# One block for all stages of a perceiver layer: what moves where when the last cross-attention steps and the self-attention units share their queues

## The chip, the core and the metric

The kernel runs on one core of one Trainium2 chip. A core has TensorE (PE, matmuls and transposes; PEld is its weight load), VectorE (DVE), ScalarE (ACT), GpSimd (POOL) and SyncE (SP, which issues the DMAs). Each engine takes its instructions strictly in the order in which they are written, and waits on semaphores between them. The metric is the device time of the whole program in microseconds (us), lower is better; three runs gave 1323.09, 1324.57 and 1327.39 us, median 1324.57.

## The reference

Two batches of 256 rows with 256 channels (`x`) attend to 4096 context rows (`ctx`), then to themselves, then pass through a gated FFN whose activations and weights are rounded to FP4 in blocks of 16.

```python
x = x + xattn(layernorm(x), ctx)    # 16 heads of 64, softmax over 4096 keys, biases, output through Wo
x = x + attn(layernorm(x))          # 16 heads of 16, 256 keys; k and v come from latent_kv @ W_up
x = x + ffn(layernorm(x))           # 256 -> 704 -> 256, silu(gate) * up, fp4 on every input
# inside attn:
latent_kv = (x @ W_k + x @ W_v) @ W_down_kv          # 64 wide
scores = (q_h . k_rec_h) / sqrt(256) * exp(-0.01 * |i - j|)
```

## The kernel before, in words

The program has two blocks, one after the other; at the end of a block every engine waits for the others.

**Block 1, `cross_attention`.** 8 groups (2 batches x 4 groups of 4 heads) of 16 steps, N = 128 steps. Step n handles one head and 1024 keys: `scores(n + 1)`, four turns (`turn`, PE transposes of the softmax numerators) and four value products (`values`), with `p_high` on ACT and `p_low` on DVE splitting each turned tile into two parts. Steps 0 to N - 5 also project keys and values for step n + 4 (`project_k`, `project_v`), which POOL then splits (`split_piece`, `split_v`); the last four steps, N - 4 to N - 1, have no projection. In these four the kernel has two `post` transposes of the last group (step N - 2) and the building of the decay table on ACT. Batch 0's rows of `y` are complete some twelve steps before the end; the last group only adds to batch 1.

Behind step N - 1, in order: `post` 2 and 3 (transposes of the last group's outputs), the combination of the self-attention's k, v and down weights (L628, L635), `turn_o` and `project_o` (L508, L517), and `add_y` on DVE (L872). This is the last merge.

**Block 2, `self_attention_and_ffn`.** Norm of all four row tiles (bn_stats on DVE, a square root on ACT, L1412), transposes and projections (`x`, `lat`, `q`, `k`, `v`, 9 visits to the PSUM tile `saP`), then U = 32 units, one per batch and head. Loop index i on PE holds `scores(i)`, `turn(i - 2)`, `values(i - 3)`; DVE multiplies by the decay and takes the maximum (L1663, L1666), ACT does exp (L1495), the copy of the turned tile (L1503) and, for units 0 to 12, the masking of q for a head (`sa_qm`, L1505). Between the units DVE and POOL round the FFN weights to FP4 in six chunks: `WEIGHT_AT` says at which unit DVE does its parts of a chunk, POOL does four tensor operations per chunk (L1112 to L1118), and `TURN_AT` says at which i PE transposes it (L1269, L1275). DVE may not start chunk c before POOL has finished chunk c - 2. Behind the units stands the FFN: gate, up, rounding chains on DVE (`round_chain`), and down. `idle` (L1197) is a matmul whose result nobody reads.

## Time and profile before

| | |
|---|---|
| median of three runs | 1324.57 us |
| the profiled execution | 1324.31 us, of which its span 1322.6 us |
| busy share of the span | PE 97%, PEld 84%, DVE 67%, ACT 67%, POOL 72% |
| cross-attention, start to last value product | 0 to about 1149.9 us |
| last merge, norm, projections | about 1149.9 to 1178.1 us |
| units | 1178.1 to about 1270.8 us |
| FFN | about 1270.8 to 1322.6 us |

The page of the profile gives busy shares over the whole span. Of those 97% most is cross-attention, so the shares say little of the stages behind it; these are read from the timeline and from the busy times of short stretches.

### The profile page before, as it was taken

How to read it: one execution, taken by the hardware profiler on the slowest of the kernel's cores; microseconds unless marked ns; L12 is line 12 of the kernel's file. 1: busy time of each engine (PE TensorE's matmuls, PEld its weight loads, DVE VectorE, ACT ScalarE, POOL GpSimd, SP SyncE). 2: the span in 40 equal slices, each digit the busy share in tenths (PEclk: the TensorE clock that was granted, in tenths of full speed). 3: DMA queues.
4: the chain of work that ended last, by engine and by line, in shares of the span. 5: the costliest groups of instructions: out<-in, count | busy, mean ns of one | idle time of the engine just before them, and what ended most of it. 6: DMA issues, size and time to landing. Idle time of an engine off the chain costs nothing. (4 is left out here: it accounts for less than half of the span.)

```text
span 1322.6 us, 25021 instructions
## 1 busy us (share of the span) xinstructions
PE 1277.8 (97%) x9210; PEld 1107.2 (84%) x9210; DVE 881.7 (67%) x1408; ACT 881.7 (67%) x1721; POOL 947.9 (72%) x1096
## 2 busy tenths in 40 slices
PE   5899999999999999999999999999999999798998
PEld 5788888888888888888888888888888888567875
DVE  3666667666766677667666676667666766748557
ACT  3677776667767666777676776666777667548641
POOL 4877897789867976788778977898779777117310
PEclk9999999999999999999999999999999999989989
DMA  4010000000001001110000000000000001200000
GB/s 135 18 41 13 17 1 9 9 17 1 9 9 33 1 17 41 41 49 1 17 1 17 1 9 10 17 1 9 9 1 1 1 9 33 72 1 1 1 1 16
DMA packets 24904, 22.97 MB, mean 17 GB/s; under 512 B 4432, under 2 KB 24528, under 8 KB 24784
## 3 DMA queue, kind: packets, MB, share of 16 engines
q1 hardware_dynamic: 24784, 21.38, 5.3%
q8 instruction: 74, 1.21, 0.4%
q14 instruction: 46, 0.38, 0.1%
HBM read 20.85 MB, written 0.52 MB: 16 GB/s over the span
## 5 line engine op out<-in xcount | busy, mean ns | idle before, releaser
L684 ACT ACTIVATE pT_hi<-psT 128x512 fp32r<-128x512 f32 x512 | 293.4, 601 | 242.9 <-PE psT L437 239.6
L774 DVE TENSOR_TENSOR pT_lo<-psT,pT_hi 128x512 fp32r<-128x512 f32 x512 | 330.1, 685 | 103.1 <-ACT pT_hi L684 102.4
L768 DVE TENSOR_REDUCE negm<-psS 128x1 f32<-128x1024 f32 x256 | 311.4, 1217 | 20.5 <-PE psS L427 16.9
L336 POOL TENSOR_TENSOR kT<-kraw,khi 64x512 fp32r<-64x512 f32 x252 | 324.0, 1286 | 0.0
L647 ACT ACTIVATE prob<-psS,negm 128x1024 f32<-128x1024 f32 x256 | 285.5, 1115 | 1.0 <-DVE negm L768 1.0
L437 PEld LDWEIGHTS psT<-ident,prob 128*128 128x128 f32 x2048 | 230.2, 141 | 65.2 <-issue 36.8
L437 PE MATMUL psT<-ident,prob 128*128 128x128 f32 x2048 | 273.5, 276 | 3.8 <-DVE pT_lo L774 3.8
L453 PE MATMUL psO<-pT_hi,v 128*128 128x256 f32 x1024 | 268.7, 295 | 2.9 <-DVE pT_lo L774 1.2
L454 PE MATMUL psO<-pT_lo,v 128*128 128x256 f32 x1024 | 256.8, 282 | 0.0
L453 PEld LDWEIGHTS psO<-pT_hi,v 128*128 128x128 f32 x1024 | 194.7, 190 | 5.3 <-DVE pT_lo L774 2.9
L427 PE MATMUL psS<-kT,q_hi 64*128 64x512 f32 x1024 | 194.8, 416 | 3.4 <-ACT prob L647 2.0
L841 DVE TENSOR_TENSOR oT<-psO,olow 64x256 f32<-64x256 f32 x128 | 53.5, 418 | 214.9 <-ACT olow L745 214.9
L454 PEld LDWEIGHTS psO<-pT_lo,v 128*128 128x128 f32 x1024 | 195.7, 191 | 0.0
L330 POOL CAST khi<-kraw 128x512 fp32r<-128x512 f32 x126 | 76.9, 611 | 163.4 <-ACT kraw L657 160.5
L348 POOL TENSOR_TENSOR v<-vraw,v 128x512 fp32r<-128x512 f32 x124 | 159.7, 1288 | 9.9
L335 POOL CAST kT<-kraw 64x512 fp32r<-64x512 f32 x252 | 153.4, 609 | 15.5
L478 PE MATMUL psW<-wv_s,ctxT_hi 128*128 128x256 f32 x1000 | 160.7, 283 | 0.0
L465 PE MATMUL psW<-ctxT_hi,wk_s 128*128 128x512 f32 x496 | 145.9, 416 | 0.7 <-DVE oweighed L854 0.6
L478 PEld LDWEIGHTS psW<-wv_s,ctxT_hi 128*128 128x128 f32 x1000 | 138.0, 192 | 0.1
L427 PEld LDWEIGHTS psS<-kT,q_hi 64*128 64x128 f32 x1024 | 96.3, 184 | 41.3 <-issue 13.1
L427 PE MATMUL psS<-kT,q_lo 64*128 64x512 f32 x512 | 101.2, 391 | 0.0
L478 PE MATMUL psW<-wv_s,ctxT_lo 128*128 128x256 f32 x500 | 100.7, 283 | 0.0
(258 smaller groups left out, 1669.1 us busy)
## 6 DMA issues: line engine op xcount, KB each, us to landing
cst<-in_ctx_dram SPq DMA_DIRECT2D x12, 512.0 KB, 3.9
wraw<-in_L_xattn_Wk_dram SPq DMA_DIRECT2D x8, 256.0 KB, 2.7
wraw<-in_L_xattn_Wv_dram SPq DMA_DIRECT2D x8, 256.0 KB, 2.7
wraw<-in_L_xattn_Wq_dram SPq DMA_DIRECT2D x8, 256.0 KB, 2.6
wo<-in_L_xattn_Wo_dram SPq DMA_DIRECT2D x8, 256.0 KB, 2.7
oT<-in_ctx_dram SPq DMA_DIRECT2D x2, 512.0 KB, 5.5
prob<-in_ctx_dram SPq DMA_DIRECT2D x2, 512.0 KB, 4.7
ff_wdn<-in_L_ffn_w_down_dram SPq DMA_DIRECT2D x1, 704.0 KB, 7.5
```

The source lines that it names most:

```text
L335: pool.tensor_copy(kT[half, m // 2 % KRING, h, 0, :], raw[own, :]).then_inc(k_split, 1)
L336: pool.tensor_tensor(kT[half, m // 2 % KRING, h, 1, :], raw[own, :], khi[own, :].bitcast(F32), ALU.subtract).then_inc(k_split, 1)
L348: pool.tensor_tensor(v[:, m % VRING, :, :, 1, :], heads, v[:, m % VRING, :, :, 0, :].bitcast(F32), ALU.subtract).then_inc(v_lo, 1)
L427: last = mm(psS[:, qt, half * PIECE:(half + 1) * PIECE], q[rows, (h + half) % 2, h // 2, qt * P:(qt + 1) * P], kT[rows, n // 2 % KRING, h ...
L437: last = pe.transpose(psT[:, t % 2, k * S + qt * P:k * S + qt * P + P], prob[:, prob_slot(n, qt), (2 * t + k) * P:(2 * t + k + 1) * P], id ...
L453: mm(psO[:, 0:S], w, pT_hi[:, at, k * S:(k + 1) * S], start=(t == 0 and k == 0), stop=False)
L454: last = mm(psO[:, 0:S], w, pT_lo[:, at, k * S:(k + 1) * S], start=False, stop=(t == TB - 1 and k == 1))
L478: last = mm(dst[:, k * GD:(k + 1) * GD], x_[:, kt, keys], wv_s[:, a, kt, :], start=(j == 0 and kt == 0), stop=(j == 2 and kt == KT - 1))
L647: act.activation(prob[:, prob_slot(n, qt), :], psS[:, qt, :], ACT.Exp, bias=negm[:, g % 2, h, qt, c:c + 1], accum_out=lsum[:, g % 2, h, qt ...
L684: act.activation(pT_hi[:, i % PRING, :], psT[:, t % 2, :], ACT.Copy).then_inc(ph_ok, 1)
L768: dve.tensor_reduce(negm[:, g % 2, h, qt, c:c + 1], psS[:, qt, :], AX.X, ALU.max, negate=True)\
L774: dve.tensor_tensor(pT_lo[:, i % PRING, :], psT[:, t % 2, :], pT_hi[:, i % PRING, :].bitcast(F32), ALU.subtract).then_inc(pl_ok, 1)
```

## The change

The two blocks become one, and the tiles of the later stages are laid over tiles of the cross-attention that are dead by then. All stages therefore stand in one queue per engine, and work is put elsewhere in these queues:

- Batch 0's input norm: statistics on DVE in steps N - 12 and N - 11, the inverse root as 14 small POOL operations (`newton`) and the normalization as two POOL operations in step N - 7 (`input_norm(0)`). No square root on ACT is left here.
- Batch 0's projections and the combination of the k, v and down weights: in steps N - 4 to N - 1, through the PSUM bank `psW`. The first two units' scores, unit 0's maximum and exp: in step N - 1.
- The last merge: `post` 2 and 3, `turn_o`, `project_o` at i = 2, 3, 5, 6 of the unit loop; `add_y` at unit 7.
- Batch 1's norm at units 8 and 9 (DVE) and inside POOL's chunk 2; its projections at i = 11 to 15.
- The masking of q is done per batch: 3 DVE operations in step N - 2, one ACT operation in step N - 1 and 28 ACT operations in the units, of 256 columns each, where there were 3 DVE and 13 ACT operations of 512 columns.
- `idle` matmuls: 17 go before and in the first units; one comes at each of i = 32, 33, 34, four before `turn_xq(1)`, two before `turn_h(3)`. `hidden(1)` stands ahead of `normalize(1)`.

The PE queue from the last value products of step N - 1 on, before (psO is the value product's bank, oT and on the last group's outputs):

```order
L453 MATMUL psO<-pT_hi,v 128x256
L454 MATMUL psO<-pT_lo,v 128x256
L500 MATMUL psW<-ident,oT 128x128 x4
L500 MATMUL psS<-ident,oT 128x128 x4
L628 MATMUL psT<-ident,sa_w 128x128 x4
L635 MATMUL psT<-sa_wd,sa_wkvT 128x64 x4
L508 MATMUL psW<-ident,on 128x128 x4
L517 MATMUL psW<-wo,oweighed 128x256 x4
L81 UNCONDITIONAL_BRANCH
```

From there to the branch that ends the block there is nothing of the units. The PE queue of step N - 1 now (L858 is batch 0's v projection, L905 unit scores, L917 unit turns, L745 `post`):

```order
L699 MATMUL psO<-pT_lo,v 128x256
L858 MATMUL psW<-sa_wu,sa_latT 128x256 x2
L682 MATMUL psT<-ident,prob 128x128 x8
L905 MATMUL saS<-sa_kT,sa_qm 128x256 x2
L682 MATMUL psT<-ident,prob 128x128 x8
L698 MATMUL psO<-pT_hi,v 128x256
...
L905 MATMUL saS<-sa_kT,sa_qm 128x256 x2
L698 MATMUL psO<-pT_hi,v 128x256
...
L699 MATMUL psO<-pT_lo,v 128x256
L905 MATMUL saS<-sa_kT,sa_qm 128x256 x2
L745 MATMUL psW<-ident,oT 128x128 x4
L917 MATMUL saT<-ident,sa_p 128x128 x4
```

The scores of units 0 and 1 stand between the turns and value products of the step, and unit 2 directly behind its last product.

The POOL queue around chunk 2 of the weights, before (ff_win are the gate and up weights):

```order
L1118 TENSOR_TENSOR ff_win<-ff_wa,ff_wamax 128x768
L1112 TENSOR_TENSOR ff_wa<-ff_win,ff_wrs 128x768
L1114 TENSOR_TENSOR ff_wa<-ff_wa,ff_wm 128x768
L1116 TENSOR_TENSOR ff_wa<-ff_wa,ff_wm 128x768
L1118 TENSOR_TENSOR ff_win<-ff_wa,ff_wamax 128x768
L1112 TENSOR_TENSOR ff_wa<-ff_win,ff_wrs 128x768
```

and now (sa_l are the norm's small tiles, cst the normalized rows of batch 1):

```order
L632 TENSOR_TENSOR ff_win<-ff_wa,ff_wamax 128x768
L621 TENSOR_TENSOR ff_wa<-ff_win,ff_wrs 128x768
L529 TENSOR_SCALAR sa_l<-sa_l 128x2
L530 TENSOR_SCALAR sa_l<-sa_l 128x2
L533 TENSOR_TENSOR sa_l<-sa_l 128x2
L535 TENSOR_TENSOR sa_l<-sa_l 128x2
...
L537 TENSOR_SCALAR sa_l<-sa_l 128x2
L539 TENSOR_TENSOR sa_l<-sa_l 128x2
L548 TENSOR_SCALAR cst<-y,sa_mv,sa_l 128x256 x2
L628 TENSOR_TENSOR ff_wa<-ff_wa,ff_wm 128x768
L630 TENSOR_TENSOR ff_wa<-ff_wa,ff_wm 128x768
L632 TENSOR_TENSOR ff_win<-ff_wa,ff_wamax 128x768
```

Fourteen small operations and the two normalizations of batch 1 stand between the first and the second operation of chunk 2.

The diff, cut to its core:

```diff
+            def input_norm(b):
+
+                rows = slice(QT * b, QT * b + QT)
+                pool.wait_ge(lguess, 2 * b + 2)
+                newton(lv[:, rows], lw[:, rows], lt[:, rows], lr[:, rows], lroot, ROOT_OPS * b)
+                pool.wait_ge(lroot, ROOT_OPS * (b + 1))
+                for r in range(QT * b, QT * b + QT):
+                    pool.tensor_scalar(s_xn[:, r, :], y[:, r, :], s_mv[:, r, 0:1], lr[:, r:r + 1], ALU.subtract, ALU.mult)\
+                        .then_inc(sxn_ok, 1)
 
...
                                        ALU.add).then_inc(bo_ok, 1)
+                if n == N - 7:
...
+                pool.tensor_tensor(blocks(a), blocks(src), wide(wrs), ALU.mult).then_inc(wp, 1)
+                if c == 0:
+                    for k in range(2, 4):
+                        add_out(GP - 1, k)
+                if c == 2:
+                    input_norm(1)
+                pool.wait_ge(wq, wq_at[c, 6])
...
 
+            dims = lambda d: slice(d * P, (d + 1) * P)
+            rows_b = lambda b: slice(b * S, (b + 1) * S)
+
+            def idle(dst, count):
+
+                for _ in range(count):
+                    mm(dst, ident[:, :], sw[:, 0, 0, :], start=True, stop=True)
+
+            def turn_x(b, dst):
+                pe.wait_ge(sxn_ok, QT * (b + 1))
...
-                elif k == 14 and g + 1 == GP:
+                elif n == N - 4:
+                    turn_x(0, psW[:, :])
+                elif n == N - 3:
+                    combine_kv()
+                elif n == N - 2:
+                    pe.wait_ge(proj_ok, projected(0, "q"))
                     post(g, 0, psW[:, :])
+                elif n == N - 1:
+                    pe.wait_ge(proj_ok, projected(0, "k"))
+                    unit_v(0, psW[:, :])
                 if n + 1 < N and visit_first(n):
...
-                if g == GP - 1 and k == 14:
+                elif n == N - 3:
+                    project_lat(0, psW[:, :])
+                elif n == N - 2:
                     wait(pe, comb, 8 * g + 1)
                     post(g, 1, psW[:, :])
+                elif n == N - 1:
+                    unit_scores(0)
                 turn(n, 2)
...
+                elif n == N - 4:
+                    turn_kv()
+                elif n == N - 3:
+                    pe.wait_ge(proj_ok, projected(0, "lat"))
+                    unit_q(0, psW[:, :])
+                elif n == N - 2:
+                    wait(pe, comb, 8 * g + 2 * 1 + 1)
+                    unit_k(0, psW[:, :])
+                elif n == N - 1:
+                    unit_scores(1)
                 if early:
...
-            pe.wait_ge(comb, 8 * (GP - 1) + 2 * 1 + 1)
-            post(GP - 1, 2, psW[:, :])
-            pe.wait_ge(exp_ok, 2 * N)
-            post(GP - 1, 3, bank_S[0])
-            pe.wait_ge(tail.kv_ok, 1)
-            pe.wait_ge(pl_ok, 4 * N)
...
-            turn_o(GP - 1)
-            project_o(GP - 1)
+            for i in range(2, U + 3):
+                if i < U:
+                    unit_scores(i)
+                if i == LATE:
+                    pe.wait_ge(proj_ok, projected(0, "v"))
+                    post(GP - 1, 2, psW[:, :])
+                if i == LATE + 1:
+                    post(GP - 1, 3, bank_S[0])
+                if i == LATE + 3:
+                    turn_o(GP - 1)
+                if i == LATE + 4:
+                    project_o(GP - 1)
+                if i < U + 2:
+                    unit_turn(i - 2)
+                if turns_at(i) is not None:
+                    turn_w(turns_at(i))
+                if i in PROJECT_AT:
+                    kind = PROJECT_AT[i]
+                    same_bank_free(kind, 1)
+                    project[kind](1, saP[:, bank_of(kind, 1), :])
+                if i == 21:
+                    turn_out(0)
...
+                if i == U - 1:
+                    turn_xq(0)
+                if i >= U:
+                    pe.wait_ge(wt_ok, NG)
+                    idle(saP[:, 0, 0:D], 1)
+                if i >= 3:
+                    unit_values(i - 3)
+
+            gate(0)
+            turn_out(1)
+            up(0)
+            project_out(1)
...
+            pe.wait_ge(x1_ok, 2)
+            idle(saO[:, 1, 0, :], 4)
+            turn_h(0)
+            down(0)
+            pe.wait_ge(eg_ok, 2)
+            idle(saT[:, 0, 0, :], 4)
+            turn_xq(1)
...
+            residual(3)
+            pe.wait_ge(eg_ok, R)
+            idle(saT[:, 0, 0, :], 2)
+            turn_h(3)
+            down(3)
...
+                elif n == N - 4:
+                    projected_out(0, "x", psW[:, :])
...
+                elif n == N - 1:
+                    projected_out(0, "v", psW[:, :])
...
+                elif n == N - 3:
+                    projected_out(0, "lat", psW[:, :])
...
+                elif n == N - 4:
+                    wait(act, tail.kvT_ps, 1)
+                    act.activation(tail.wkvT[:, :, :].rearrange("p t n -> p (t n)"), psW[:, :], ACT.Copy)\
+                        .then_inc(tail.kvT_ok, 1)
+                elif n == N - 3:
+                    projected_out(0, "q", psW[:, :])
+                elif n == N - 2:
+                    projected_out(0, "k", psW[:, :])
+                elif n == N - 1:
+                    unit_exp(0)
                 wait(act, av_ok, 4 * n + 4)
...
-            o_out(GP - 1)
+                if n == N - 2:
...
+            for u in range(1, U + 2):
+                if u == LATE + 3:
+                    o_out(GP - 1)
+                if turns_at(u) is not None:
+                    weight_out(turns_at(u))
+                if u in PROJECT_AT:
+                    kind = PROJECT_AT[u]
+                    projected_out(1, kind, saP[:, bank_of(kind, 1), :])
+                if u < U:
+                    unit_exp(u)
+                if u >= 2:
+                    unit_turned_out(u - 2)
+                if u + 3 < U:
...
+                if n == N - 1:
+                    unit_max(0)
...
+                if n in (N - 12, N - 11):
+                    input_statistics(n - N + 12)
+                if n == N - 10:
+                    input_guess(0)
+                if n == N - 2:
+                    for i in range(3):
+                        own_rows(i)
                 out_sum(n)
...
-            for k in range(2, 4):
-                weigh_out(GP - 1, k, psW[:, :] if k == 2 else bank_S[0])
-                add_out(GP - 1, k)
-            add_y(GP - 1)
...
-            cols = lambda d: slice(d * P, (d + 1) * P)
-            idle(psO[:, 1, 0, :], 7)
-            pe.wait_ge(xn_ok, R)
-            for kt in range(KT):
-                step(("x", kt), turn_x(kt))
-            pe.wait_ge(proj_ok, at[("x", 1)] + 1)
-            pe.wait_ge(wc_ok, 1)
-            step(("lat", 0), product([(wc[:, kt, :], xnT[:, kt, :]) for kt in range(KT)]))
-            pe.wait_ge(w_in[2], 16)
...
-                if i in (2, 3):
-                    idle(psO[:, 1, 0, :], 5 if i == 2 else 1)
...
-                if i == 3:
-                    idle(psO[:, 1, 0, :], 4)
-                if i >= 3:
-                    values(i - 3)
...
+                if u >= 1:
+                    unit_max(u)
+                if u in (LATE, LATE + 1):
+                    weigh_out(GP - 1, u - LATE + 2, psW[:, :] if u == LATE else bank_S[0])
                 for c, op in weight_ops(u):
                     weight_op(c, op)
+                if u == LATE + 5:
+                    add_y(GP - 1)
+                if u in (LATE + 6, LATE + 7):
+                    input_statistics(QT + u - LATE - 6)
+                if u == LATE + 7:
+                    input_guess(1)
...
             round_chain(CHAIN_H[0], hh[:, 0, :], range(5))
             statistics(1)
             round_chain(CHAIN_H[0], hh[:, 0, :], range(5, 9))
+            hidden(1)
             normalize(1)
             dve.wait_ge(fxn_ok, 4)
             round_chain(CHAIN_X, input_rows(1), range(10))
-            hidden(1)
             round_chain(CHAIN_H[1], hh[:, 1, :], range(9))
```

## Rows read from the trace of the kernel before

**Rows 1.** Stretch, its us; busy PE, PEld, DVE, ACT, POOL; PEclk; DMA share; GB/s.

```profile
1150.90:1162.20 11.30, 7.38 (x32) 5.41 (x32) 4.25 (x7) 1.71 (x4) 0.00 (x0) 0.71 0.00 0
...
1189.10:1215.20 26.10, 23.08 (x161) 20.29 (x160) 22.75 (x64) 20.55 (x58) 18.83 (x13) 1.00 0.01 2
...
1270.80:1275.40 4.60, 4.60 (x11) 2.51 (x11) 0.75 (x2) 0.00 (x0) 0.00 (x0) 0.54 0.00 0
```

**Rows 2.** PE timeline, end of step N - 1: start, duration, line, operation.

```profile
1149.65 0.28 PE L454 MATMUL psO<-pT_lo,v 128*128 128x256 f32 x1
```

**Rows 3.** PE timeline, projections and scores of unit 2.

```profile
1170.76 3.70 PE L1180 MATMUL saP<-sa_xnT,sa_w 128*128 128x512 f32 x8
...
1180.33 1.10 PE L1232 MATMUL saS<-sa_kT,sa_qm 128*128 128x256 f32 x4 [0.21 <-DVE sa_top L1663]
```

**Rows 4.** PE timeline, waits inside steps N - 4, N - 2, N - 1.

```profile
1123.84 1.26 PE L437 MATMUL psT<-ident,prob 128*128 128x128 f32 x8 [0.98 <-DVE pT_lo L774]
...
1142.31 0.39 PE L453 MATMUL psO<-pT_hi,v 128*128 128x256 f32 x1 [0.78 <-DVE pT_lo L774]
...
1145.99 1.26 PE L437 MATMUL psT<-ident,prob 128*128 128x128 f32 x8 [1.47 <-DVE pT_lo L774]
```

**Rows 5.** PE timeline, units: scores, turn, values, scores of units 8, 17.

```profile
1197.37 1.11 PE L1232 MATMUL saS<-sa_kT,sa_qm 128*128 128x256 f32 x4
1198.32 0.60 PE L1242 MATMUL saT<-ident,sa_p 128*128 128x128 f32 x4
...
1199.08 0.96 PE L1253 MATMUL saO<-sa_v,sa_pT 128*128 128x16 f32 x8
1199.89 1.11 PE L1232 MATMUL saS<-sa_kT,sa_qm 128*128 128x256 f32 x4
...
1225.16 1.11 PE L1232 MATMUL saS<-sa_kT,sa_qm 128*128 128x256 f32 x4
```

**Rows 6.** POOL timeline, cross-attention's last steps.

```profile
1117.13 0.61 POOL L330 CAST khi<-kraw 128x512 fp32r<-128x512 f32 x1 [1.73 <-ACT kraw L657]
...
1138.70 0.72 POOL L387 TENSOR_TENSOR oweighed<-oweighed 128x256 f32<-128x256 f32 x1 [12.17 <-DVE oweighed L854]
```

**Rows 7.** POOL timeline, first and last of 14 root operations.

```profile
1249.72 0.23 POOL L1125 TENSOR_SCALAR ff_w<-ff_v 128x2 f32<-128x2 f32 x1 [13.65 <-DVE ff_r L1622]
...
1253.44 0.20 POOL L1135 TENSOR_TENSOR ff_r<-ff_r,ff_t 128x2 f32<-128x2 f32 x1
```

**Rows 8.** POOL timeline, last operation of chunk 2.

```profile
1209.77 1.49 POOL L1118 TENSOR_TENSOR ff_win<-ff_wa,ff_wamax 128x768 f32<-128x768 f32 x1
```

**Rows 9.** DVE timeline, one small operation alone, one beside POOL's.

```profile
1182.25 0.19 DVE L1569 TENSOR_SCALAR ff_wrs<-ff_wamax 128x48 f32<-128x48 f32 x1
...
1199.65 1.79 DVE L1569 TENSOR_SCALAR ff_wrs<-ff_wamax 128x48 f32<-128x48 f32 x1
```

**Rows 10.** POOL timeline, the operation beside it.

```profile
1199.58 1.81 POOL L1116 TENSOR_TENSOR ff_wa<-ff_wa,ff_wm 128x768 f32<-128x768 f32 x1
```

**Rows 11.** PE timeline, last value products, gate and up matmuls.

```profile
1267.89 3.14 PE L1253 MATMUL saO<-sa_v,sa_pT 128*128 128x16 f32 x16
1270.87 4.68 PE L1313 MATMUL saP<-ff_wgT,ff_xqT 128*128 128x512 f32 x8
...
1275.82 2.53 PE L1313 MATMUL saS<-ff_wgT,ff_xqT 128*128 128x512 f32 x8
...
1295.02 4.30 PE L1313 MATMUL saT<-ff_wgT,ff_xqT 128*128 128x512 f32 x8 [0.34 <-ACT ff_xqT L1460]
```

**Rows 12.** DVE timeline, first and third hidden product.

```profile
1278.45 0.89 DVE L1688 TENSOR_TENSOR ff_h<-saS,ff_eg 128x704 f32<-128x704 f32 x1 [6.57 <-PE saS L1313]
...
1301.79 0.89 DVE L1688 TENSOR_TENSOR ff_h<-saS,ff_eg 128x704 f32<-128x704 f32 x1 [1.73 <-PE saS L1313]
```

**Rows 13.** Groups by line, 1178 to 1323: count, busy us, mean ns, idle before.

```profile
L1663 DVE CUSTOM_DVE_ANT_0 sa_s<-saS,sa_decay 128x256 f32<-128x256 f32 x64 | 24.1, 414 | 25.0 <-PE saS L1232 24.7 <-ACT sa_p L1495 0.2
...
L1578 DVE TENSOR_SCALAR ff_wm<-ff_wm 128x704 f32<-128x704 f32 (+2 forms) x12 | 6.3, 521 | 0.4
```

1305 lines of the change are left out of this document (636 added, 669 removed).

## The prediction

> **What bounds the kernel now.** I read four views. First the busy times by stretch. Over the cross-attention PE is the bound and the change touches none of its full steps, so their 1120 us stay. Between its end and the units lies a stretch in which no engine is full: in the 11.3 us of 1150.9 to 1162.2 PE is busy 7.38 us at a granted clock of 0.71 (part of it at 1.2 GHz), DVE 4.25, ACT 1.71, POOL not at all [rows 1]. That is a serial chain: transpose, weigh, transpose, project, norm, project. Then PE's timeline: the last value product of the cross-attention starts at 1149.65 and is issued by 1149.9 [rows 2]; the scores of unit 2 start at 1180.33 [rows 3]. The third view is PE's waits inside the last four steps, which say how much can be put there for nothing [rows 4]. The fourth is the rhythm of the units: without a wait a unit with a weight turn takes 1199.89 - 1197.37 = 2.52 us of PE: scores 0.95, seven transposes 0.76, values 0.81 [rows 5]. Ten units take 1225.16 - 1197.37 = 27.8 us, 2.78 each [rows 5], and PE is idle 3.0 of the 26.1 us from 1189.1 [rows 1]. So in the units PE is close to the bound, and what is added to its queue there is paid nearly in full.
>
> **Gain 1: the serial stretch.** Now unit 2's scores stand directly behind the last value product. Falls away: 1180.33 - 1149.9 = 30.4 us. Everything that stood there is paid elsewhere, in the next terms.
>
> **Cost 1: the last four steps.** Prices: a matmul record of 512 columns takes 3.70/8 = 0.46 us [rows 3], so one of 256 columns 0.23; a transpose 0.76/7 = 0.11 [rows 5]. Added on PE: x 4 transposes 0.43; k and v weights 4 transposes 0.43; their combination, 8 records of 64 columns that I price like a transpose, 0.9; lat 4 records 0.92; q 8 records 1.84; k and v 0.92 each; two scores 1.9. Sum 8.3 us. The steps have waits for this: 0.98 us ahead of the third turn in N - 4, 0.78 ahead of a value product in N - 2, 1.47 ahead of the third turn in N - 1 [rows 4]. Step by step: in N - 4 x stands ahead of the first turn and delays its whole chain, 0.5; the weights' transposes add 0.2. In N - 3 the combination stands ahead of the first turn, 0.8; lat falls into the wait; q stands before the third value product and about 0.8 of it comes through. In N - 2 k (0.92) against a wait of 0.78, and the ACT copy and DVE's three maskings are behind what PE needs: 0.3. In N - 1 v must wait for ACT's copy of k, and ACT's copy of v stands ahead of the first `p_high`, while unit 0's scores go into the wait: 0.5. Together 3.1 us. Bounds: 0.9 (only v is seen) to 8.3 (nothing is hidden).
>
> POOL's norm of batch 0 in step N - 7 is priced at nothing. Fourteen root operations run from 1249.72 to 1253.64, 3.9 us [rows 7]. No row shows a POOL normalization of 128x256; a tensor product of that size takes 0.72, a cast of 128x512 takes 0.61 [rows 6], so one lies between 0.3 and 0.72, and I take 0.7, the row that reads as much per element as it can. Together 5.3 us, against 1.73 us of idle time per step [rows 6]. The rest is a shift of 3.6 us of `split_piece` and `split_v` that is worked off in two steps. ACT's next copy into `vraw` is some 4 us behind the split that frees it, so this cover is thin: were it gone, ACT and PE would be late by 1 to 2 us once.
>
> **Cost 2: units 2 to 6.** Before they take 1197.37 - 1180.33 = 17.0 us, of which ten `idle` matmuls go. Now PE has 5 x 2.2 us of own work, `post` 2 x 0.43, `turn_o` 0.43, `project_o` 8 x 0.23 = 1.84: 14.1 us. DVE needs 1.0 for a unit's maximum (two products of 0.41 and a small operation of 0.19), some 0.8 for a weighing (two operations of that size) and 1.1 to 1.5 for its part of a chunk (0.52 for an operation over a whole chunk) [rows 9, 13], with one wait for POOL about 2.7 us per unit, and values(0) has to wait for exp(2). I take 16.6: 0.4 us won. Bounds: 14.1 (2.9 won) and 17.0 + 3.1 (3.1 lost).
>
> DVE's small operations are the risk there. One of 48 columns takes 1.79 us while POOL's product of 1.81 us runs [rows 9, 10]; alone the same line takes 0.19 [rows 9]. One such wait per chunk is in my 2.7 us. The Trainium skill (SBUF — State Buffer, on the engine side and the shared port pair) says that GpSimd and a DVE operation in a two-port mode hold the pair as an exclusive lock and the other fully blocks. By that rule POOL's two added normalizations and four partial sums would hold DVE up as well; the trace agrees for this pair of rows. It is a rival below, by its own price.
>
> **Cost 3: units 7 to 16.** Five projections of batch 1 on PE: 0.43 + 0.92 + 1.84 + 0.92 + 0.92 = 5.0 us. And a new wait: `turn_x(1)` at i = 11 needs POOL's norm, which starts when DVE has done unit 9 with its statistics and guess. From the end of scores(9), DVE needs a maximum 1.0, chunk 2's two operations 1.1, statistics and guess about 1.0 (one operation of 256 columns and three small ones) [rows 9, 13], POOL then 5.4: 8.5 us. PE in the same time has one unit and the scores and turns of i = 11, 5.0 to 6 us. Queued behind this wait are unit 8's values and unit 12's scores, so nothing passes it: about 3 us. Behind it POOL is 5.4 us late with chunk 2, whose last operation ended at 1211.26 [rows 8], just when DVE took chunk 4; DVE now stands there, and unit 12's maximum behind it. By then PE has q(1) to do, so most of that is covered: 0.7. Some 2 of the 3.0 us that PE is idle before [rows 1] lie here; the projections fill 1.4 of them. Sum 5.0 + 3.0 + 0.7 - 1.4 = 7.3 us. Bounds: 5.0, and 5.0 + 5.4 = 10.4.
>
> **Units 17 to 31:** the same PE queue as before. ACT gets a masking per unit, behind the copy that PE waits for and ahead of an exp that waits for DVE anyway: nothing.
>
> **Gain 2: the tail.** From 1270.8 the granted clock is 0.54 [rows 1], nearly all of it the lower level, after a stretch in which PE waited and issued only 16-column matmuls. There 16 value records take 3.14 us where 8 take 0.96 [rows 11, 5], and gate(0) takes 4.68 and gate(2) 4.30 us where the up matmuls of the same form take 2.53 at 2.4 GHz [rows 11]. If the added `idle` matmuls keep the clock, hidden(0), now at 1278.45, comes 1.2 + 2.15 earlier, less 0.9 for the three `idle` (two records each, one of them in a wait): 2.5. The third hidden product waits 1.73 us [rows 12] for gate(2) and up(2); of the 1.77 saved I count 1.5, since `hidden(1)` now stands ahead of the second norm. Sum 4.0. Bounds: 4.0, and -1.6 if the clock falls anyway and all `idle` are in the way. What no run here can show: the skill (TensorE: Matmul & The Clock Gate, HAM oscillation) holds that activity releases the throttle, so that dummy work pays.
>
> **The sum** against the profiled execution, 1324.3 us (span 1322.6 and 1.7 around it), 0.3 under the median: 30.4 - 3.1 + 0.4 - 7.3 + 4.0 = 24.4 us. 1324.3 - 24.4 = 1299.9; I say 1300. All best bounds: 30.4 - 0.9 + 2.9 - 5.0 + 4.0 = 31.4, 1293. All worst: 30.4 - 8.3 - 3.1 - 10.4 - 1.6 = 7.0, 1317.
>
> **Rivals.**
> - *DVE and POOL bound the first half of the units* (0.18). For it: the 1.79 us row, and DVE 22.75 us busy in 26.1 [rows 1] before it gets anything more. Against: the weighings and norms sum to only 5 us over nine units. Two further port waits of 1.6 and costs 1 and 3 nearer their far ends: 5 to 9 us less gain, 1305 to 1309.
> - *The clock in the tail falls all the same* (0.14). For it: `idle` comes one at a time between 16-column products. The 4.0 become -0.5 (0.9 for three `idle`, 0.4 won on DVE): 1304.5.
> - *More is hidden* (0.07): the four steps cost 1.5 and units 2 to 6 run at PE's pace: 1.6 + 2.5 us better, 1296 or less.
> - *PE falls to 1.2 GHz inside the units* (0.03), and the kernel gets slower. Place: the wait at i = 11, after the `idle` matmuls that stood at the units' start are gone. For it: after the broken stretch from 1150.9 the clock was 0.71 [rows 1]. Against: waits of 1 us and more from 1189.1 on left it at 1.00 [rows 1]. Price: 2.2 to 2.5 us more per unit, the PE work again. From 24.4/2.3, about 11 units at the low clock, the change loses; all 21 behind i = 11 give 1300 + 48 = 1348, half of them 1324. By the skill's page on the clock gate a long enough gap does this; the time by it is the one just worked out.
>
> **How the numbers follow.** My forecast, 1300, holds 0.58, with 1296 to 1304 as its own range. The range 1294.5 to 1309 takes in the clock rival, nearly all of the first one and half of the better one; outside remain about 0.15. The measurement of this kernel can tell 0.3%, 4 us, from no change: faster than 1320.6 has 0.95, within 0.02, slower 0.03 (the last rival, most of it).
>
> **What would show it.** Right: PE's last value product of step N - 1 near 1153, unit 2's scores within 0.3 us behind it, unit 7's near 1170, unit 17's near 1205; a PE wait of 2 to 4 us at i = 11 released by POOL's normalization; a granted clock near 1.00 at gate(0) and gate(2), with 2.5 us each. Wrong: unit 2's scores later than 1158 (the steps hide less), DVE and not PE waited for in units 2 to 10 with unit 11 later than 1187, or a clock under 0.9 within the units.

## The result and the profile after

The changed kernel takes 1311.28 us (median of five runs, 1310.36 to 1315.8) against 1324.24 us before (five runs, 1323.09 to 1327.39). The ratio is 0.9906, 95% interval 0.9885 to 0.9927: faster by 13.0 us, where 24.4 us were forecast, and outside the range (1294.5 to 1309). The profiled execution has a span of 1309.2 us against 1322.6, so 13.4 us of the difference can be followed in it.

First the busy times by stretch, which answer to [rows 1]. The columns are busy us (instructions) of each engine, the granted clock and the DMA share; the stretches run from unit 2's scores to unit 4's, to unit 6's, to unit 11's, to unit 13's (with the wait at i = 11), to unit 17's, and from unit 31's scores to `hidden(0)`.

```profile
1154.65:1162.70 8.05, 4.92 (x34) 3.92 (x32) 7.23 (x25) 4.66 (x14) 2.68 (x3) 1.00 0.01 2
1162.70:1170.80 8.10, 8.10 (x38) 7.16 (x37) 7.75 (x18) 4.69 (x15) 7.43 (x6) 0.58 0.00 0
1170.80:1187.00 16.20, 14.65 (x101) 12.97 (x100) 12.91 (x43) 10.94 (x34) 8.09 (x9) 1.00 0.00 1
1187.00:1199.00 12.00, 8.28 (x45) 6.51 (x45) 2.75 (x11) 5.13 (x15) 10.91 (x17) 0.86 0.00 0
1199.00:1213.20 14.20, 14.20 (x90) 12.04 (x90) 11.24 (x33) 10.63 (x30) 9.61 (x7) 1.00 0.01 2
1253.40:1266.40 13.00, 12.91 (x80) 10.32 (x80) 2.06 (x8) 7.40 (x17) 0.00 (x0) 1.00 0.01 1
```

The serial stretch is gone, but the granted clock is 0.58 where units 4 and 5 stand, 1.2 GHz for most of it, and 0.86 in the stretch with the wait at i = 11. Over all the units before (1178 to 1270.8) it was 0.99, and 1.00 up to 1262. DVE is 7.23 of 8.05 and 7.75 of 8.10 us busy.

PE's timeline (start, duration; in brackets the idle time ahead and who ended it), at the places of [rows 2 to 5] and [rows 11]:

```profile
1128.09 0.63 PE L877 MATMUL psW<-ident,sa_w 128*128 128x128 f32 x4 [1.62 <-POOL sa_w L608]
...
1154.65 1.03 PE L905 MATMUL saS<-sa_kT,sa_qm 128*128 128x256 f32 x4
...
1157.50 1.10 PE L905 MATMUL saS<-sa_kT,sa_qm 128*128 128x256 f32 x4 [0.60 <-DVE sa_top L1668]
...
1161.85 1.04 PE L932 MATMUL saO<-sa_v,sa_pT 128*128 128x16 f32 x8 [2.38 <-ACT sa_pT L1271]
1162.74 1.85 PE L905 MATMUL saS<-sa_kT,sa_qm 128*128 128x256 f32 x4
...
1166.80 2.05 PE L905 MATMUL saS<-sa_kT,sa_qm 128*128 128x256 f32 x4
...
1174.82 1.11 PE L905 MATMUL saS<-sa_kT,sa_qm 128*128 128x256 f32 x4
...
1186.95 1.11 PE L905 MATMUL saS<-sa_kT,sa_qm 128*128 128x256 f32 x4
...
1192.64 0.63 PE L826 MATMUL saP<-ident,cst 128*128 128x128 f32 x4 [3.72 <-POOL cst L548]
...
1194.15 2.05 PE L905 MATMUL saS<-sa_kT,sa_qm 128*128 128x256 f32 x4
...
1213.23 1.11 PE L905 MATMUL saS<-sa_kT,sa_qm 128*128 128x256 f32 x4
...
1253.41 1.11 PE L905 MATMUL saS<-sa_kT,sa_qm 128*128 128x256 f32 x4
...
1261.15 2.61 PE L991 MATMUL saP<-ff_wgT,ff_xqT 128*128 128x512 f32 x8
...
1283.29 2.60 PE L991 MATMUL saT<-ff_wgT,ff_xqT 128*128 128x512 f32 x8 [0.34 <-ACT ff_xqT L1293]
```

L877 is `turn_kv` in step N - 4, L905 a unit's scores (1154.65 is unit 2, 1157.50 is 3, 1162.74 is 4, 1166.80 is 5, 1174.82 is 7, 1186.95 is 11, 1194.15 is 12, 1213.23 is 17, 1253.41 is 31), L932 value products, L826 `turn_x(1)`, L991 the gate and up matmuls. Scores take 1.11 us at 2.4 GHz and 2.05 at 1.2.

DVE, at the places of [rows 9] and [rows 12]: L1671 is the small operation that ends a unit's maximum, L1569 one of a chunk's small ones, L1796 `hidden(0)`.

```profile
1159.02 0.94 DVE L1671 TENSOR_SCALAR sa_negm<-sa_top 128x2 f32<-128x2 f32 x1
...
1165.44 1.19 DVE L1671 TENSOR_SCALAR sa_negm<-sa_top 128x2 f32<-128x2 f32 x1
...
1166.75 1.78 DVE L1569 TENSOR_SCALAR ff_wrs<-ff_wamax 128x48 f32<-128x48 f32 x1
...
1266.68 0.89 DVE L1796 TENSOR_TENSOR ff_h<-saS,ff_eg 128x704 f32<-128x704 f32 x1 [4.51 <-PE saS L991]
```

ACT's copy that the wait at i = 3 is for (L1271) behind the exponential of unit 2 (L1263), and POOL (the places of [rows 6 to 8] and [rows 10]):

```profile
1160.50 0.49 ACT L1263 ACTIVATE sa_p<-sa_s,sa_negm 128x256 f32<-128x256 f32 x1
...
1161.11 0.60 ACT L1271 ACTIVATE sa_pT<-saT 128x512 f32<-128x512 f32 x1
```

```profile
1126.67 1.27 POOL L608 TENSOR_TENSOR sa_w<-sa_w 128x512 f32<-128x512 f32 x1
...
1166.68 1.81 POOL L630 TENSOR_TENSOR ff_wa<-ff_wa,ff_wm 128x768 f32<-128x768 f32 x1
...
1190.05 2.44 POOL L548 TENSOR_SCALAR cst<-y,sa_mv,sa_l 128x256 f32<-128x256 f32 x2
```

L608 is the sum of the k and v weights, L628 and L630 are the sum and the difference in a chunk's rounding (the recorded texts call them products), L548 the normalization of batch 1. The starts put side by side (before from [rows 3], [rows 5], [rows 12] and, for unit 31, this row of the kernel before):

```profile
1262.72 1.11 PE L1232 MATMUL saS<-sa_kT,sa_qm 128*128 128x256 f32 x4
```

| place | before | after | earlier by | forecast |
|---|---|---|---|---|
| unit 2's scores | 1180.33 | 1154.65 | 25.7 | 27.3 |
| unit 7's scores | 1197.37 | 1174.82 | 22.5 | 27.7 |
| unit 17's scores | 1225.16 | 1213.23 | 11.9 | 20.4 |
| unit 31's scores | 1262.72 | 1253.41 | 9.3 | 20.4 |
| `hidden(0)` | 1278.45 | 1266.68 | 11.8 | 22.9 |
| span | 1322.6 | 1309.2 | 13.4 | 24.4 |

The tail gave what was forecast. Of the 11 us that are missing, 1.6 went in the last steps, 3.6 in units 2 to 6, 3.3 in units 7 to 16 and 2.6 in units 17 to 31.

### The profile page after: what moved, and what is told of

Same layout as the page of the kernel before. It is cut to its first block, busy times and chain, and to the rows that moved or that the text cites. A ratio compares the mean times of both kernels' runs of the same rounds, so it can differ in the third digit from the quotient of the medians.

```text
span 1309.2 us, 25086 instructions
## 1 busy us (share of the span) xinstructions
PE 1269.7 (97%) x9210; PEld 1104.8 (84%) x9210; DVE 879.5 (67%) x1405; ACT 881.6 (67%) x1735; POOL 961.1 (73%) x1132
## 4 chain that ended last, share of the span: by engine, by line
PE 86%; POOL 7%; DVE 4%; ACT 2%; issue 2%; DMA 0%; POOLq 0%; ACTq 0%; DVEq 0%
PE psT L682 17%; PE psS L672 14%; PE psW L710 13%; PE psW L723 12%; PE psO L698 9%; PE psO L699 9%; POOL kT L510 2%; PE saS L905 1%; PE saO L932 1%; PE psW L762 1%; PE saO L1036 1%; PE psW L732 1%; PE psW L745 1%; POOL kT L509 1%; PE psW L738 1%
## 5 line engine op out<-in xcount | busy, mean ns | idle before, releaser
L1448 DVE TENSOR_REDUCE negm<-psS 128x1 f32<-128x1024 f32 x256 | 311.6, 1217 | 20.8 <-PE psS L672 17.3
L509 POOL CAST kT<-kraw 64x512 fp32r<-64x512 f32 x252 | 153.4, 609 | 15.5
L672 PEld LDWEIGHTS psS<-kT,q_hi 64*128 64x128 f32 x1024 | 96.6, 185 | 41.4 <-issue 13.4
```

The lines of the kernel that those rows point to most:

```text
L509: pool.tensor_copy(kT[half, m // 2 % KRING, h, 0, :], raw[own, :]).then_inc(k_split, 1)
L672: last = mm(psS[:, qt, half * PIECE:(half + 1) * PIECE], q[rows, (h + half) % 2, h // 2, qt * P:(qt + 1) * P], kT[rows, n // 2 % KRING, h ...
L1448: dve.tensor_reduce(negm[:, g % 2, h, qt, c:c + 1], psS[:, qt, :], AX.X, ALU.max, negate=True)\
```

## Experiments

Each kernel was timed in alternation with the kernel before on the same chip; the ratio is to it, with its 95% interval. The batches are e1 to e4, e5 to e8, e9 to e12, e13 to e16, and e17 with e18. Kernels of one batch can be compared by their medians to some 0.5 us. The changed kernel was timed beside the others only in the last batch; a gain on it that is given in us for another batch is the difference of two medians of different batches (the kernel before had 1323.2 to 1324.6 in them), and is good to about 1.5 us. Of each kernel one execution was traced. Where a unit is said to come so many us after another, that is between the starts of their scores in PE's timeline. All edits are to the changed kernel if nothing else is said.

### The wait in step N - 4 (e1)

```diff
+            wait(pool, tail.w_in[0], 16)
+            wait(pool, tail.w_in[1], 16)
+            pool.tensor_tensor(tail.w[:, 0, :, :], tail.w[:, 0, :, :], tail.w[:, 1, :, :], ALU.add).then_inc(tail.kv_ok, 1)
             pool.memset(tail.win[:, :, tail.win.shape[2] - 1, :], 0.0).then_inc(tail.zero_ok, 1)
...
-            wait(pool, tail.w_in[0], 16)
-            wait(pool, tail.w_in[1], 16)
-            pool.tensor_tensor(tail.w[:, 0, :, :], tail.w[:, 0, :, :], tail.w[:, 1, :, :], ALU.add).then_inc(tail.kv_ok, 1)
```

> POOL adds the two key weights (L608) ahead of its small memsets and masks instead of behind them, so about 1.5 us earlier. Theory POOL-late (the norm of batch 0 on POOL is worked off too slowly and comes out at PE's turn_kv in step N-4, which waited 1.62 us for this sum): the wait goes, steps N-4 onward come 1.4 to 1.6 us earlier and the whole kernel gains about 1.4 us on the changed kernel (1311.3 to 1309.9). Rival, the steps are held by the chain through ACT and DVE and the wait for the sum only stands in front of a later wait: the wait goes from the rows, the next scores come at most 0.3 us earlier and the time stays within 0.5 us.

1309.35 us, 0.9879 (0.9845 to 0.9914). PE's timeline of e1, `turn_kv` without a wait, and `project_o` (L762):

```profile
1126.37 0.63 PE L877 MATMUL psW<-ident,sa_w 128*128 128x128 f32 x4
...
1171.14 2.56 PE L762 MATMUL psW<-wo,oweighed 128*128 128x256 f32 x8
```

Unit 2's scores stand at 1152.98 instead of 1154.65, so 1.7 us are won there: the wait was real and not in front of another. But unit 17's come only 0.6 us earlier (1212.6): PE was at 1.2 GHz up to unit 6 (scores of 2.05 us in units 5 and 6), and unit 7 stood at 1174.79 against 1174.82. The interval holds both theories; the timeline decides for the first.

### PE's clock (e2, e3, e7, e11)

```diff
+                if i == 3:
+                    idle(saP[:, 1, 0:D], 8)          # e7: 5
                 if i >= 3:
                     unit_values(i - 3)
```

> Eight idle products of 256 columns (8 x 0.23 = 1.84 us) go into the wait of 2.38 us ahead of values(0) at i=3, into a bank that nobody reads. Theory clock (PE at 1.2 GHz from 1162.7 to 1170 costs 0.74+0.46+0.76+0.94+0.46+0.14 = 3.5 us against the same rows at 2.4 GHz): units 4 and 5 run at full clock, unit 7's scores come 2.5 to 3.5 us earlier and the kernel gains as much. Rival chain (DVE works without a gap from 1155.3 to 1171.1, so PE's slowness is hidden behind it): the clock is back at 1.00, but unit 6's maximum comes at most 1 us earlier and the time gains 0 to 1 us.

```diff
                     same_bank_free(kind, 1)
+                    if kind == "x":
+                        idle(saP[:, bank_of(kind, 1), 0:D], 12)          # e7: 7
                     project[kind](1, saP[:, bank_of(kind, 1), :])
```

> Twelve idle products of 256 columns (2.8 us) go into the wait of 3.72 us for POOL's norm at i=11. Theory clock: the wait's end stays where it is, scores(12) take 1.11 instead of 2.05, the turn behind them 0.60 instead of 1.06, values 1.06 instead of 1.20: 1.5 us gained, 1.3 to 1.6 at the end. Rival chain (unit 12's maximum is held by POOL's late chunk 2 until 1198.6 whatever PE does): the clock is back, and 0 to 0.5 us are gained.

e2: 1310.04 us, 0.9885 (0.985 to 0.9919). e3: 1311.76 us, 0.99 (0.9865 to 0.9935). Both fills were twice as long as meant, since I had taken an idle product for one record of 0.23 us: it is two. In e2 they ended about 1 us after the copy was there, in e3 about 1.6 us after the norm; with the clock back e2 still brought unit 7 to 18.5 us behind unit 2 (20.2 in the changed kernel) and won 1.0 us up to unit 17, e3 0.2 us. So they were run again at their right size, together.

> The two fills again, now as long as the waits: an idle product is two records, so 0.45 us (16 records took 3.62 us), five at i=3 make 2.26 us of 2.38, seven at i=11 make 3.17 of 3.72. Theory clock: no stretch at 1.2 GHz in the units; 2 to 3.5 us at i=3 and 1.5 at i=11, together 3.5 to 5 us faster than the changed kernel. Rival chain (DVE and POOL set the pace behind both waits): 0 to 1 us.

1308.78 us, 0.9882 (0.9849 to 0.9916): 2.5 us better than the changed kernel, less than the clock theory wants and more than its rival. PE's timeline of e7:

```profile
1165.23 1.11 PE L905 MATMUL saS<-sa_kT,sa_qm 128*128 128x256 f32 x4
...
1168.59 1.06 PE L932 MATMUL saO<-sa_v,sa_pT 128*128 128x16 f32 x8 [1.37 <-ACT sa_pT L1275]
...
1170.53 3.50 PE L762 MATMUL psW<-wo,oweighed 128*128 128x256 f32 x8
```

The first fill keeps the clock in units 4 and 5, and unit 7 still comes 20.2 us after unit 2, as without it: PE then waits 1.37 us for ACT, behind a maximum that DVE ended late, and falls to 1.2 GHz one unit later (`project_o`, L762, 3.50 us instead of 1.89). In e2, whose longer fill held PE back, that wait was 0.53 us and the clock did not fall. The second fill wins: unit 13 comes 10.3 us after unit 11 (1196.53 and 1186.23), 12.0 without it.

> The kernel before, without its ten idle products at units 2 and 3 (the seven ahead of turn_x stay). Theory clock: with the wait for unit 0's copy empty PE falls to 1.2 GHz in units 4 and 5 here too, unit 7's scores come 2 to 3.5 us later relative to unit 2's and the kernel is that much slower, 1326.5 to 1328. Rival: the idle products only filled a wait, or stood in the way; 0 to 1 us either way.

1324.4 us, 1.0012 (0.9991 to 1.0032): no difference that this interval can tell, and none of the forecast size is shown. PE's timeline of the kernel before without its ten idle products:

```profile
1157.01 1.97 PE L517 MATMUL psW<-wo,oweighed 128*128 128x256 f32 x8 [1.02 <-ACT oweighed L690]
...
1177.99 1.10 PE L1232 MATMUL saS<-sa_kT,sa_qm 128*128 128x256 f32 x4 [0.21 <-DVE sa_top L1659]
...
1183.94 1.04 PE L1253 MATMUL saO<-sa_v,sa_pT 128*128 128x16 f32 x8 [2.31 <-ACT sa_pT L1499]
...
1188.47 2.05 PE L1232 MATMUL saS<-sa_kT,sa_qm 128*128 128x256 f32 x4
...
1196.38 1.11 PE L1232 MATMUL saS<-sa_kT,sa_qm 128*128 128x256 f32 x4
```

The clock falls as forecast (2.05 us for unit 5's scores), and from unit 2 (1177.99) to unit 7 (1196.38) it takes 18.4 us where 17.0 were needed with them: 1.4 us lost, less than the forecast 2 to 3.5, since 4.5 us of PE work went with the ten products. At the end of the traced execution this does not show (span 1321.9 us against 1322.6), because unit 2 came 2.3 us earlier than in the kernel before: in the last merge `project_o` (L517), which the edit does not touch, took 1.97 us; in the kernel before it took 3.75:

```profile
1157.48 3.75 PE L517 MATMUL psW<-wo,oweighed 128*128 128x256 f32 x8 [1.02 <-ACT oweighed L690]
```

So the idle products did keep the clock, and without them PE falls to 1.2 GHz behind a wait of 2.31 us in this kernel too.

### DVE beside POOL (e9, e16, e17, e18, e13)

```diff
-                dve.tensor_scalar(s_negm[:, u, :], top[:, u, :], -1.0, None, ALU.mult).then_inc(smax_ok, 1)
+                dve.tensor_tensor(s_negm[:, u, :], plain[:, 0:2], top[:, u, :], ALU.subtract).then_inc(smax_ok, 1)
...
-                    dve.tensor_scalar(rs, amax, 1.0 + 2.0 ** -23, None, ALU.mult).then_inc(done, 1)
+                    dve.tensor_tensor(rs, amax, plain[:, 2:3].to_broadcast([P, nb]), ALU.mult).then_inc(done, 1)
```

> The changed kernel with two of DVE's small operations in another form: the negation of a unit's maxima (L1671) as zero minus the maxima, and the scale of a chunk's blocks (L1569) as a product with a constant, both between two tensors instead of a tensor and a number. Theory port: a DVE operation of the tensor-and-number form waits while a POOL product runs (0.94, 1.19, 1.78, 1.11, 1.47 us instead of 0.17 to 0.19 in units 2 to 7), one between two tensors does not; the waits go, DVE's chain through units 2 to 8 gets 3 to 5 us shorter, the kernel is 3 to 5 us faster than the changed one. Rival: the wait belongs to the small size or to the place and stays, or moves to the next operation (L1567, L1575): 0 to 1 us.

1310.71 us, 0.9907 (0.9893 to 0.9922), as the changed kernel. The theory that the form decides, so stated, falls: the same operation between two tensors waits as well. DVE in e9:

```profile
1164.88 0.93 DVE L1675 TENSOR_TENSOR sa_negm<-plain,sa_top 128x2 f32<-128x2 f32 x1
...
1165.94 1.83 DVE L1572 TENSOR_TENSOR ff_wrs<-ff_wamax,plain 128x48 f32<-128x48 f32 x1
```

The same edit was made to e6 (below).

> The same new form on top of e6_swap_norm7 (1298.3 us), where DVE works nearly without a gap from 1153.9 to 1183 with about 6.7 us of such waits in it. Theory port: the wait of 1.52 us at unit 10's scores and the half clock behind it (1.7 us) go, and what POOL's chain has left of room shows: 3 to 5 us faster than e6, 1293.5 to 1295.5. Rival: 0 to 1 us.

1298.52 us, 0.9814 (0.98 to 0.9828), against 0.9802 for e6: nothing either.

Instead of the form, the POOL operations beside them were cut to 16 columns of 768. This kernel leaves out the rounding of the rest of chunks 0 and 1:

```diff
+                if c < 2:
+                    src, a, m, nb = src[:, 0:BLOCK], a[:, 0:BLOCK], m[:, 0:BLOCK], 1
                 pool.wait_ge(wq, wq_at[c, 6])
```

> The changed kernel with POOL's last three products of chunks 0 and 1 on 16 columns instead of 768 (the rest of these two chunks is left unrounded). Theory port (DVE's small operations stand still while a POOL product runs: 0.4 + 1.0 + 1.6 + 0.2 us in units 3 to 5 and 0.9 + 1.3 in unit 7): the rows of L1671, L1569 and L1578 fall to 0.17, 0.19 and 0.56 us, unit 7's scores come 2.5 to 4 us earlier, unit 11's 4 to 6, the kernel is 4 to 6 us faster than the changed one. Rival, DVE's own work is too much: 0 to 1 us. Between them: POOL itself is earlier with chunk 2, which alone would move only units 12 and later.

1310.83 us, 0.9909 (0.9891 to 0.9926): no gain in the time. DVE in e16, units 4 and 5:

```profile
1165.26 0.42 DVE L1670 CUSTOM_DVE_ANT_0 sa_s<-saS,sa_decay 128x256 f32<-128x256 f32 x1 [1.12 <-PE saS L907]
...
1166.07 0.17 DVE L1673 TENSOR_SCALAR sa_negm<-sa_top 128x2 f32<-128x2 f32 x1
...
1166.36 0.19 DVE L1571 TENSOR_SCALAR ff_wrs<-ff_wamax 128x48 f32<-128x48 f32 x1
...
1169.53 0.42 DVE L1670 CUSTOM_DVE_ANT_0 sa_s<-saS,sa_decay 128x256 f32<-128x256 f32 x1 [2.49 <-PE saS L907]
```

In these units the waits beside POOL are gone (L1673 and L1571 are L1671 and L1569 of the other kernels, 0.17 and 0.19 us), as the port theory says; but DVE now waits 1.12 and 2.49 us for PE, which runs at 1.2 GHz, and unit 7 comes 21.8 us after unit 2. Behind them the edit does win: units 7 to 10 take 10.2 us, 12.1 in the changed kernel.

How much of such a time is the clock can be added up. The last column but one is what PE's rows of units 2 to 6 at 1.2 GHz took longer than the same rows at 2.4 GHz:

| kernel | unit 2 to unit 7 | low clock | without it |
|---|---|---|---|
| changed | 20.2 | 3.5 | 16.7 |
| e1 | 21.8 | 5.2 | 16.6 |
| e9 | 18.5 | 1.8 | 16.7 |
| e16 | 21.8 | 5.2 | 16.6 |

All four have the same wait of 2.38 us at i = 3, and the whole difference between them is how long PE stayed at 1.2 GHz behind it. DVE's waits beside POOL, absent in units 4 and 5 of e16 alone, change nothing here as long as PE is slow. They show when it is not: in e7 they end the maximum late and bring on the next fall. So e16 lost 1.6 us to a longer low stretch, won 2.0 behind it and lost 1.7 more in units 11 to 16, where PE was slow for longer too; its time alone says little against the port theory. That calls for both edits at once.

> The changed kernel with the short POOL products of e16 (chunks 0 and 1 stay mostly unrounded) and the five idle products of e7 in unit 3. Theory two locks: in e7 PE had its clock and waited for DVE, in e16 DVE had no waits and waited for a slow PE, each alone held units 2 to 7 at 20.1 to 21.7 us; with both gone they take 15.5 to 17 us, and 3 to 4 us of it reach the end, 1307.5 to 1308.5. Rival, something third holds them (ACT's copy behind the exponential): 19 us or more and less than 1.5 us at the end.

> The changed kernel unaltered, as the measure for e17: 1310 to 1312 us, 0.990 to 0.992 of the kernel before.

e17: 1307.16 us, 0.987 (0.9852 to 0.9888). e18, the changed kernel: 1312.15 us, 0.9912 (0.9897 to 0.9927); the execution that was traced took 3135 us, so no row of it is used. Together the two edits win 5.0 us (3 to 4 were expected), where e16 alone had won nothing and e7, with the fill at i = 11 besides, 2.5. PE in e17, unit 7's scores, 17.3 us behind unit 2's (1154.95), near the theory's 15.5 to 17 and far from its rival's 19:

```profile
1172.22 1.11 PE L907 MATMUL saS<-sa_kT,sa_qm 128*128 128x256 f32 x4
```

The waits at i = 3 and i = 5 are down to 0.22 and 0.17 us, the clock does not fall, and unit 11 comes 27.4 us after unit 2 instead of 32.3.

Last, the form once more, as a reduction, on e6:

```diff
-                dve.tensor_scalar(s_negm[:, u, :], top[:, u, :], -1.0, None, ALU.mult).then_inc(smax_ok, 1)
+                dve.tensor_reduce(s_negm[:, u, :], top[:, u, :].unsqueeze(2), AX.X, ALU.max, negate=True)\
+                    .then_inc(smax_ok, 1)
```

> e6_swap_norm7 with the negation of a unit's maxima as a reduction over one element; reductions, reciprocals and the maximum itself show no wait beside POOL's products in any trace. Theory form: L1671 always takes 0.17 us, the wait moves to the next scalar operation (L1567, L1569), which nobody but the chunk needs, ACT gets unit 2's, 4's and 7's maxima 0.8 to 1.2 us earlier; 0.5 to 2 us faster than e6. Rival place: the reduction waits as the two other forms did (e9, e10), 0 us.

1299.75 us, 0.9826 (0.9811 to 0.9841), against 0.9802 for e6: no gain. But the form's theory holds this time. DVE in e13:

```profile
1162.71 0.15 DVE L1671 TENSOR_REDUCE sa_negm<-sa_top 128x2 f32<-128x2 f32 x1
1162.78 1.34 DVE L1567 TENSOR_SCALAR ff_wamax<-ff_wamax 128x48 f32<-128x48 f32 x1
```

The reduction takes 0.15 us while the POOL operation of 1.81 us (L628) runs, and the next scalar operation takes the wait of 1.34. Unit 7 comes 2.0 us earlier than in e6, and then the guess of batch 1's norm meets the POOL operations instead (its two small operations take 0.78 and 1.42 us), PE waits 2.62 us for DVE at unit 10's scores, falls to 1.2 GHz, and the gain is given back.

### The order of ACT and the place of the norm (e5, e4, e6, e12, e14, e15)

```diff
-                if u < U:
-                    unit_exp(u)
                 if u >= 2:
                     unit_turned_out(u - 2)
+                if u < U:
+                    unit_exp(u)
```

> ACT copies a unit's turned weights (L1271) before the next-but-one unit's exponential instead of behind it. Theory queue: PE's value products wait for that copy, the copy stands behind an exponential that waits for DVE's maximum, so PE is tied to DVE's newest unit; with the copy first the waits of 2.38, 0.33, 1.22, 0.97, 0.49 and 0.44 us in the units go, and with the first one the half clock behind it (up to 3.5 us): 4 to 8 us faster than the changed kernel. Rival DVE: DVE works without a gap from 1155.3 to 1171.1, so PE will wait for DVE at the scores instead (their tile is free when the maximum two units back is done); 0 to 1.5 us.

1307.63 us, 0.9867 (0.9829 to 0.9905). The waits for the copy are gone but for 0.38 us, and unit 11 comes 29.2 us after unit 2 instead of 32.3. Then PE waits 5.87 us for the norm (first fence below) and stays at 1.2 GHz through unit 13, so that unit 17 comes 61.5 us after unit 2 instead of 58.6. What is won is won behind it: units 17 to 31 take 35.7 us instead of 40.2.

```diff
-                if u in (LATE + 6, LATE + 7):
-                    input_statistics(QT + u - LATE - 6)
-                if u == LATE + 7:
+                if u == LATE + 5:
+                    input_statistics(QT)
+                    input_statistics(QT + 1)
                     input_guess(1)
```

> Batch 1's statistics and guess all stand right behind add_y at unit 7 instead of at units 8 and 9; POOL, idle from 1181.5 to 1186.0, can norm from about 1182.4 to 1188. Theory norm wait: turn_x(1) no longer waits (3.72 us), the half clock behind it goes (1.5 us), chunk 2 is no longer late on POOL; DVE's 1.6 us of statistics ahead of unit 8's maximum cost up to 1.7 us back, so 3 to 5 us gained. Rival (DVE is the bound of these units): unit 8's to 10's maxima come 1.6 us later and keep so, the gain is 1.5 to 2.5 us. Third: the end of units 11 to 16 is held by the projections alone and the wait had hidden DVE's and POOL's other lateness: under 1 us.

1309.67 us, 0.9889 (0.9847 to 0.9931); its six runs lie between 1306.3 and 1316.1, so that its gain is uncertain. The wait at i = 11 is gone, but a new one of 2.95 us stands at i = 9, for ACT's copy behind the exponential of unit 8, whose maximum DVE now takes after the statistics, with a fall of the clock behind it. Unit 12 comes 40.4 us after unit 2, with the late norm it was 39.5. Each edit alone leads into another wait with a fall of the clock behind it; e6 has both, and e1's.

> Three edits at once: ACT's copy before the exponential, batch 1's statistics and guess at unit 7, the key weights' sum ahead of POOL's memsets. Theory queue: DVE's lateness by the statistics no longer reaches PE, so the wait of 3.72 us at i=11 goes and with it its half clock; with e5's gain and the 1.5 us of the sum 9 to 13 us faster than the changed kernel, 1298 to 1302. Rival DVE: 1.5 us of the sum and about 2 us more, 1307 to 1308.

1298.25 us, 0.9802 (0.9766 to 0.9838): 13 us better than the changed kernel, within the theory's 1298 to 1302. By the medians the three edits alone gave 1.9 (e1), 1.6 (e4) and 3.7 us (e5), together 7.2. PE's timeline of e5, e4 and e6 at these places:

```profile
1191.24 1.09 PE L826 MATMUL saP<-ident,cst 128*128 128x128 f32 x4 [5.87 <-POOL cst L548]
...
1193.69 2.05 PE L905 MATMUL saS<-sa_kT,sa_qm 128*128 128x256 f32 x4
```

```profile
1185.80 1.07 PE L932 MATMUL saO<-sa_v,sa_pT 128*128 128x16 f32 x8 [2.95 <-ACT sa_pT L1271]
...
1190.98 2.05 PE L905 MATMUL saS<-sa_kT,sa_qm 128*128 128x256 f32 x4
```

```profile
1179.15 1.91 PE L905 MATMUL saS<-sa_kT,sa_qm 128*128 128x256 f32 x4 [1.52 <-DVE sa_top L1668]
...
1185.63 0.63 PE L826 MATMUL saP<-ident,cst 128*128 128x128 f32 x4
```

Units 17 to 31, which had lost 2.6 us, take 36.0 us in e6, 37.6 before and 40.2 in the changed kernel: these, too, were waits for the copy.

e12 moves `turn_o` and `project_o` to the end of units 5 and 6 and has five idle products ahead of unit 10's scores.

> e6_swap_norm7 with turn_o and project_o of the last merge at the end of units 5 and 6 instead of behind their scores (their waits of 0.85 and 1.28 us go), and five idle products ahead of unit 10's scores, where PE waits for DVE. Theory DVE: DVE has no gap until 1183, so only the half clock behind unit 10's scores is won: 1.2 to 1.9 us faster than e6, 1296.5 to 1297. Rival PE: the two waits come through as well, 3 to 4 us, 1294.5 to 1295.

1299.3 us, 0.9821 (0.9809 to 0.9834), as e6. PE is 1.1 us earlier at unit 11 and then waits 1.23 us for POOL's norm; both theories fall, the norm sets this place.

e14 is e6, but in unit 7 puts `add_y`, statistics and guess ahead of `weight_ops(u)`, has `2: (7, 8, 10)` in `WEIGHT_AT`, and `input_norm(1)` ahead of chunk 2's first product on POOL, with three idle products at i = 11. e15 adds e12's order and e13's reduction.

> As e6, but in unit 7 add_y, the statistics and the guess stand ahead of chunk 2's operations, which move from units 5, 7, 9 to 7, 8, 10, and POOL norms batch 1 ahead of chunk 2's first product; three idle products (1.4 us) go into what is left of the wait at i=11. Theory norm: what sets units 11 to 16 is the end of POOL's norm, 1185.5 in e6; it comes 2.4 to 3.4 us earlier and the kernel with it, 1295 to 1296. Rival: chunk 2, 3 us later, holds DVE at unit 12 and PE at its turns; 0 to 2 us slower than e6.

> e14 with the reduction of e13 and with turn_o and project_o at the end of units 5 and 6. With the norm out of the way the two waits of 0.85 and 1.28 us should now count: 1 to 3 us faster than e14, 1293 to 1295. Rival (as in e12, where the same order brought nothing since POOL's norm still set unit 11): within 0.5 us of e14.

e14: 1298.05 us, 0.9815 (0.98 to 0.983). e15: 1297.32 us, 0.9809 (0.9794 to 0.9824). In e15 unit 11 comes 26.2 us after unit 2, where e6 needs 30.7, and the norm ends at 1182.97 instead of 1185.49, though e15's unit 2 stands 0.9 us later; but unit 17 comes 50.3 after unit 2 against 51.8. The rest is given back at units 12 and 13, where PE waits for DVE (0.77) and for chunk 2 (0.33) and does batch 1's projections. e14 missed its theory's 1295 to 1296 and lies with its rival (0 to 2 us slower than e6, by the ratios 1.7), and e15's 0.7 us on e14 is near its rival's 0.5: the norm was earlier by what was forecast, but it no longer sets what follows. e6, e14 and e15 beat both kernels.

### The tail (e8)

The added `idle` products at i = 32 to 34, ahead of `turn_xq(1)` and of `turn_h(3)` are left out, `hidden(1)` stands behind the second norm.

> The tail as before the change: the added idle products behind unit 31, ahead of turn_xq(1) and ahead of turn_h(3) are left out, hidden(1) stands behind the second norm again. Theory clock: gate(0) takes 4.7 us and gate(2) 4.3 instead of 2.6, the kernel is 4.0 us slower than the changed one (1315.3). Rival: the clock holds here without them, since the units before them end otherwise now: within 1.5 us.

1315.57 us, 0.9925 (0.9895 to 0.9954): 4.3 us slower than the changed kernel, 4.0 were expected. PE in e8, gate(0) and gate(2):

```profile
1261.87 4.73 PE L991 MATMUL saP<-ff_wgT,ff_xqT 128*128 128x512 f32 x8
...
1286.07 4.30 PE L991 MATMUL saT<-ff_wgT,ff_xqT 128*128 128x512 f32 x8 [0.34 <-ACT ff_xqT L1286]
```

## Why the prediction was wrong

**Gain 1** holds: 30.4 us of serial work went.

**POOL's norm of batch 0, priced at nothing**, cost. The text named the cover as thin and looked for its end at ACT's copy into `vraw`; it came out at the sum of the k and v weights behind POOL's last split. The norm took 6.5 us and not 5.3, and the splits behind it started 4.8, 3.1 and 1.4 us later than before in three successive steps, where the text had the shift worked off in two. The sum started at 1125.25 before and at 1126.67 now, 1.4 us late, and PE waited 1.62 us. The step failed because I checked one consumer of POOL's queue and not the one that the change itself had put on PE's path.

**Cost 1** was 4.7 us and not 3.1. By the starts of the steps' scores (1120.19, 1127.72 and 1135.24 before, 1120.12, 1129.59 and 1138.97 after) step N - 4 took 1.9 us more (0.7 forecast) and N - 3 1.9 (1.6); N - 2 and N - 1 took about 0.4 and 0.6 (0.3 and 0.5). Nearly all of the error is the wait above (e1).

**Cost 2** was the step that failed most: units 2 to 6 took 20.2 us, forecast 16.6. The wait for exp(2) was in the sum, and the clock behind it was put at nothing. Missing is the 1.2 GHz behind the 2.38 us: 0.74 and 0.94 us on two scores, 0.46 on a unit's turn and on `turn_o`, 0.76 on the values and 0.14 on the turn behind them, together 3.5. Without it these units took 16.7 us, and the same in e1, e9 and e16. That this is the forecast number is in part luck: waits of 3.0 us for 2.5 and own work of 13.7 for 14.1 nearly cancel. The going of ten `idle` products had been booked as less PE work alone; e11 shows that it brings the fall with it. DVE's waits beside POOL cost these units nothing while PE is slow (e16) and bring on another fall once it is not (e7); with both gone the kernel wins 5.0 us (e17).

**Cost 3** was 10.6 us, forecast 7.3. The new wait took 3.72 instead of 3.0, because a POOL normalization of 128x256 takes 1.22 us and not the 0.7 of which I wrote that it read as much as it could; the half clock behind the wait took 1.5 us (0.94 on unit 12's scores, the rest on the turn and the values) that I had only in the last rival, as a catastrophe of many units and not as one unit's price; and the waits for ACT's copy that I had filled with projections (1.4 us) stood at i = 8 and 9 (0.33 and 1.22 us), ahead of them. The 0.7 us for POOL's late chunk 2 did not come: PE has no idle time from 1199.0 to 1213.2. The projections themselves were right: lat, q, k and v on 1.0, 1.7, 1.1 and 1.1 us, with `turn_x` 5.3, forecast 5.0.

**Units 17 to 31** were priced at nothing and cost 2.6 us, in waits of 0.97, 0.49 and 0.44 us for ACT's copy and in small gaps. The masking was "behind the copy that PE waits for", but that copy is behind an exponential that waits for DVE, and DVE was later than before: unit 17's maximum was complete 3.8 us behind the start of its scores, 2.4 before. In e6 it was 4.2, yet with the copy first these units take 36.0 us.

**Gain 2** was right: 4.1 us against 4.0, with gate(0) and gate(2) at 2.6 us each, and 4.3 in e8.

**The rivals.** "DVE and POOL bound the first half of the units" named 1305 to 1309 and came nearest; its mechanism was there, but it did not make this loss: without DVE's waits units 2 to 6 were no faster (e16). "PE falls to 1.2 GHz inside the units" came true for three passes of the loop, with a chance of 0.03, since I had tied it to a loss of the whole gain; [rows 4] and the waits of 1 us that had left the clock at 1.00 were shorter than the 2.38 and 3.72 us here. The Trainium skill (TensorE: Matmul & The Clock Gate, HAM oscillation) says that waits between short bursts of matmuls throttle the array anew each time; the trace agrees for two of them, with 0.58 behind the wait of 2.38 us and 0.86 for the stretch with that of 3.72. Of my marks "unit 11 later than 1187" missed by 0.05 us (1186.95) and "a clock under 0.9" was met.

## What to carry to other kernels

Before an idle product or a wait is removed, price the clock behind the next wait of 2 us and more, as a unit or two of PE work at double length, and not only as a far rival. How long PE stays slow behind the same wait differed by 3.4 us between kernels here, so take it out of two traces before a difference between them is read. On an engine that works in order, what another engine waits for belongs ahead of what itself waits: the exchange of two lines on ACT, with the norm and the weights' sum moved to match, was worth 13 us, the fills alone at most 2.5 (e7). Where two obstacles run side by side, a run that removes one can show nothing; run the pair before a theory is dropped.

## What the hardware showed

A small DVE operation stands still to the end of a POOL operation if it is of the tensor-and-number form (1.78 us for 48 columns, to within 0.05 us of the end of POOL's) or between two SBUF tensors (1.83 us, e9), and does not if it is a reduction (0.15 us beside an operation of 1.81, e13). The Trainium skill (SBUF — State Buffer, Who interferes with whom) says that a `tensor_scalar` can enter a two-port mode and then contends with GpSimd, that a DVE instruction with two SBUF inputs contends with a GpSimd instruction that reads SBUF, and that a `tensor_reduce` on trn2 never contends. The trace agrees with all three, by the numbers just given.

The time at 1.2 GHz after the same wait is not the same: behind 2.38 us of waiting it cost PE 3.5 us in the changed kernel, 1.8 in e9 and 5.2 in e1 and e16. In the changed kernel PE was back at 2.4 GHz within the turn of i = 5, in e1, whose units start 1.7 us earlier, only within `project_o` of i = 6 (L762 took 2.56 us there, 1.89 in the changed kernel). What sets that is left open here: it would take several traced executions of one kernel.
